# Gathering each run of 128 edges once in the three graph-attention passes of a GNN

## The reference, cut to what matters

```python
def _L1_gnn_ref(h, W, att, src, dst):
    z = jnp.einsum('nd,hdf->nhf', h, W)                 # 4 heads of 64
    es, ed = ...                                        # one score per node and head
    e = jax.nn.leaky_relu(es[src] + ed[dst], SLOPE)
    e = jnp.where(e == 0.0, NEG, e)
    m = jax.ops.segment_max(e, dst, num_segments=N)
    ex = jnp.exp(e - m[dst])
    denom = jax.ops.segment_sum(ex, dst, num_segments=N)
    alpha = ex / safe
    out = jax.ops.segment_sum(alpha[:, :, None] * z[src], dst, num_segments=N)

def _gat_layer(x, src, dst, W, a_src, a_dst, b, num_nodes):   # L2a: 4 heads, L2b: 1 head
    h = (x @ W).reshape(num_nodes, H, C)
    logits = jax.nn.leaky_relu(al_s[src] + al_d[dst], 0.2)
    alpha = _segment_softmax(logits, dst, num_nodes)
    out = jax.ops.segment_sum(h[src] * alpha[:, :, None], dst, num_segments=num_nodes)
```

## Time and profile before

| what | value |
|---|---|
| time, median of three runs | 3641.38 us (3639.26 to 3641.59) |
| the profiled execution: span of its instructions | 3626.7 us |
| time outside the span, by the difference | 14.7 us |
| instructions | 45,558 |
| VectorE (DVE), GpSimd (POOL) busy | 1987.0 us (55%), 2230.6 us (62%) |
| ScalarE (ACT) busy | 1393.1 us (38%) |
| gathers: L1, L2a, L2b together (L690 from t_z) | 1248, mean 984 ns |
| gathers of L3, of L0 | 416, 392 |
| moved by DMA | 389.14 MB, mean 107 GB/s |
| place loads (`dsthot`, four passes) | 416 of 128 KB |

### The profile page before, as it was taken

One profiled execution on the slowest core, in us unless ns is written; L12 is line 12 of the kernel. 1 busy time (PEld: TensorE's weight loads), 2 busy tenths in 40 slices (PEclk: granted clock), 3 DMA queues, 4 the chain that ended last, 5 costly groups with the idle time before them and its releaser, 6 DMA issues.

```text
span 3626.7 us, 45558 instructions
## 1 busy us (share of the span) xinstructions
PE 2379.2 (66%) x9551; PEld 1641.7 (45%) x9551; DVE 1987.0 (55%) x7379; ACT 1393.1 (38%) x3670; POOL 2230.6 (62%) x2460
## 2 busy tenths in 40 slices
PE   5655556838777774667777624554556588888888
PEld 2323334724444442344444424444454356555567
DVE  4554446536666673566666813333345366666677
ACT  2444544413333343333333513333343244444444
POOL 5666663566676657666766356666644366666636
PEclk7677677955666677666666755555555789999999
DMA  6656654234444423344444122222212255555411
GB/s 198 176 173 169 172 173 135 63 107 113 114 115 115 114 68 101 108 114 114 116 115 113 26 44 45 47 47 45 47 36 74 74 154 154 155 155 154 148 53 49
DMA packets 247934, 389.14 MB, mean 107 GB/s; under 512 B 58944, under 2 KB 161366, under 8 KB 247673
## 3 DMA queue, kind: packets, MB, share of 16 engines
q0 software_dynamic: 92032, 230.64, 24.6%
q1 hardware_dynamic: 155641, 155.59, 14.0%
HBM read 331.11 MB, written 54.91 MB: 106 GB/s over the span
## 4 chain that ended last, share of the span: by engine, by line
PE 39%; issue 21%; DVE 15%; another core or an unknown queue 14%; POOL 4%; ACT 3%; DVEq 2%; DMA 1%; SPq 0%; POOLq 0%; ACTq 0%
PE PS L1798 20%; PE PS L1719 6%; PE PS L1690 4%; DVE ACC L1323 3%; PE PS L1852 3%; POOL work L690 2%; DVE ACC L1090 1%; DVE work L1294 1%; PE PS L1776 1%; POOL rstd L579 1%; DVEq L376 1%; PE PS L1835 1%; PE PS L1748 1%; PE PS L1769 1%
## 5 line engine op out<-in xcount | busy, mean ns | idle before, releaser
L690 POOL DMA_INDIRECT work<-t_z,srcK x1248 | 1228.2, 984 | 610.8 <-issue 302.5
L1798 PE MATMUL PS<-work,M 128*128 128x260 f32 (+3 forms) x3328 | 1303.0, 512 | 447.6 <-issue 229.0
L1798 PEld LDWEIGHTS PS<-work,M 128*128 128x128 f32 x3328 | 757.4, 270 | 672.1 <-issue 480.2
L1323 DVE TENSOR_TENSOR ACC<-ACC,PS 128x260 f32 (+3 forms) x1614 | 588.7, 365 | 212.7 <-PE PS L1798 117.6
L2026 ACT ACTIVATE M<-iota,dloc 128x128 f32<-128x128 f32 x1248 | 396.9, 389 | 665.3 <-PE PS L1798 308.4
L690 POOL DMA_INDIRECT work<-t_x,srcK x416 | 394.0, 947 | 269.5 <-PE PS L1798 142.2
L690 POOL DMA_INDIRECT work<-in_x,srcTile x392 | 374.8, 956 | 212.2 <-issue 103.7
L1690 PE MATMUL PS<-work,M 128*128 x832 | 313.0, 519 | 240.8 <-issue 120.0
L1690 PEld LDWEIGHTS PS<-work,M 128*128 128x128 f32 x832 | 187.5, 250 | 361.5 <-issue 338.6
L1294 DVE TENSOR_TENSOR work<-work 128x256 f32<-128x256 f32 x800 | 329.1, 412 | 22.4 <-issue 14.2
L1719 PE MATMUL PS<-Y,w 128*128 x832 | 282.3, 425 | 72.2 <-issue 34.8
(11 more groups left out here) (266 smaller groups left out, 2928.9 us busy)
## 6 DMA issues: line engine op xcount, KB each, us to landing
work<-t_dhot SPq DMA_DIRECT2D x416, 128.0 KB
t_hot<-M SPq DMA_DIRECT2D x104, 256.0 KB
M<-t_hot SPq DMA_DIRECT2D x104, 256.0 KB
work<-t_z,srcK POOLq DMA_INDIRECT x1248
t_dhot<-work SPq DMA_DIRECT2D x104, 128.0 KB
work<-t_edge SPq DMA_DIRECT2D x104, 64.0 KB
work<-t_x,srcK POOLq DMA_INDIRECT x416
t_z<-Y SPq DMA_DIRECT2D x50, 130.0 KB, 2.0
```

Source lines behind the costliest of these rows:

```text
L690: pool.indirect_dma_start(out=slots[:, j, 0:width], out_offset=None, in_=table[:, :], in_offset=bass.IndirectOffsetOnAxis(ap=sources[:, k: ...
L1323: ins = vec.tensor_tensor(sums, sums, PS[k % SUMS[stage]][:, 0:cols], ALU.add)
L1798: mm(PS[k % n][:, 0:cols], M[:, k % (4 * G), :], slots_of[:, k % RING[stage], 0:cols], start=True, stop=True)\
```

## The change

- Each tile is gathered once in L1, L2a and L2b: 392 gathers a pass in place of 416, with the index table of tiles (`srcTile`) that L0 already uses. The ring of 48 slots now holds tiles.
- Rows stay raw in the ring. The tile's slot of a step is data, so VectorE, ScalarE and GpSimd load 16 slot numbers of a group into registers (`load_rows`, table `rowI`), read the row through them, and write the scaled row to a place of its own: one of three rows `sent` (where the weights w1 and w2 lay), or of 12 in the last 32 steps of L1 and L2a. Whoever writes such a row waits for the sum that read it (`wait_sent`). The weights of the softmax and the highest logits get tiles of their own (`alphas`, `tops`), and VectorE copies a step's highest logits into the sent row (`put_tops`), for which TensorE waits at each step of L2a and L2b.
- The source scores of a group are copied by ScalarE from the 16 rows into a tile (`take_sources`), after it has loaded the number of the last quad of tiles that the group needs; VectorE's second logit operation waits for that copy in place of the landing.
- SP passes on the landing of each four tiles (`relay_tiles`, tiles_ready) and, nine quads behind, that four slots are free (tiles_freed), once the steps in a table (`freeI`) are scaled. GpSimd waits for the latter once in four gathers.
- ScalarE issues the loads of `dsthot`, which SP did.
- A row is now 4 scores and four parts of 64 features and a one (264 wide), or 1 score and one part (66). The weighted ones give the denominators, so they need no fade of their own. The self-loop of L2a writes to `joined`.
- The setup makes the tables: four matmuls and one for `freeI`, and some seven small VectorE operations.

```diff
         slotI = Yf[0:1, late + PADDED + STEPS:late + PADDED + 2 * STEPS].bitcast(I32)
...
+        SENDS, SENDS_LATE = 3, 12
...
+        sent = w12[:, 0:SENDS * (SENT + HEADS)].rearrange("p (s c) -> p s c", s=SENDS)
...
-        WIDTH = {"L0": D, "L1": D, "L2a": D, "L2b": HID, "L3": D}
-        EXTRAS = {"L1": HEADS, "L2a": 2 * HEADS, "L2b": 2, "L3": 1}
+        WIDTH = {"L0": D, "L1": SENT, "L2a": SENT, "L2b": PART, "L3": D}
+        EXTRAS = {"L1": 0, "L2a": HEADS, "L2b": 1, "L3": 1}
+        TOPPED = ("L2a", "L2b")
...
+        def load_rows(eng, g):
+            _, values = nc.values_load_multi_w_load_instructions(
+                rowI[0:1, GS * g:GS * (g + 1)], engines=(eng.engine,), min_val=0, max_val=RING["L1"] - 1,
+                skip_runtime_bounds_check_because="the table was made from the steps' numbers")
+            return values
...
+        def sent_row(stage, k):
+            late = k - (STEPS - HELPED)
+            if late < 0 or stage == "L2b":
+                return sent[:, k % SENDS, :]
+            j = late % SENDS_LATE
+            return ring[:, FREE_SLOT + j, :] if j < SENDS_LATE - SENDS else sent[:, j - (SENDS_LATE - SENDS), :]
...
+        def wait_sent(eng, stage, k):
+            late = k - (STEPS - HELPED)
+            if late < 0 or stage == "L2b":
+                if k >= SENDS:
+                    eng.wait_ge(step_summed.sem, step_summed.at(stage, k - SENDS + 1))
...
+                eng.wait_ge(row_scaled.sem, row_scaled.at(stage, STEPS - HELPED))
...
+        LOT = each_of(SUMMING, G)
+        GATHERS = {**each_of(SUMMING, PADDED), "L3": STEPS}
...
+                sources = srcK if stage == "L3" else srcTile
...
-                    elif k >= many:
+                    elif k >= many and stage == "L3":
                         pool.wait_ge(step_summed.sem, step_summed.at(stage, k - many + 1))
+                    elif k >= many and k % G == 0:
+                        pool.wait_ge(tiles_freed.sem, tiles_freed.at(stage, (k - many) // G + 1))
...
+            def relay_tiles(stage):
+                for q in range(QUADS):
+                    landed(sp, stage, G * q)
+                    sp.sem_inc(tiles_ready.sem, 1)
+                    m = q - BEHIND
+                    if 0 <= m < FREED:
+                        steps = sp.value_load(freeI[0:1, m:m + 1], min_val=1, max_val=STEPS)
+                        sp.wait_ge(row_scaled.sem, steps + row_scaled.at(stage, 0))
+                        sp.sem_inc(tiles_freed.sem, 1)
...
-                        if c >= 4 and stage == "L3":
+                        if c >= 4:
                             sp.wait_ge(dsthot_made.sem, dsthot_made.at("L3", c - 3))
-                        elif c >= 4:
-                            sp.wait_ge(picked.sem, picked.at(stage, G * (c - 3)))
                         sp.dma_start(dsthot[:, c % 4, :], t_dhot[:, c * ROW:(c + 1) * ROW])\
                             .then_inc(dsthot_moved[c % 4].sem, 16)
...
+            sp.wait_ge(slots_made.sem, 3)
+            relay_tiles("L1")
+            store("L1", [(t_z2, lambda b, v: at_block(Y, b)[:, HEADS:BODY + SENT])], 1)
...
-                        landed(dve, stage, GS * g)
+                        dve.wait_ge(sources_taken.sem, sources_taken.at(stage, g + 1))
                         previous(1)
-                        ins = vec.tensor_tensor(by_step(L), by_step(A), ring[:, slot:slot + GS, width:width + heads], ALU.add)
...
+                def put_tops(k):
+                    g, i = divmod(k, GS)
+                    if i == 0:
+                        dve.wait_ge(tops_put.sem, tops_put.at(stage, g + 1))
+                    wait_sent(dve, stage, k)
+                    vec.tensor_copy(sent_row(stage, k)[:, width:width + heads], tops[:, g % 2, i * heads:(i + 1) * heads])\
+                        .then_inc(tops_sent.sem, 1)
                 def scale(k):
-                    j = k % RING[stage]
-                    if k % GS == 0:
-                        dve.wait_ge(alphas_put.sem, alphas_put.at(stage, k // GS + 1))
+                    g, i = divmod(k, GS)
+                    if i == 0:
+                        placed[0] = load_rows(dve, g)
+                        dve.wait_ge(alphas_put.sem, alphas_put.at(stage, g + 1))
+                    if helper(stage, k) != "vector":
+                        return
+                    wait_sent(dve, stage, k)
+                    row, o = ring_row(placed[0][i])[:, heads:heads + width], sent_row(stage, k)[:, 0:width]
                     if heads > 1:
-                        z = ring[:, j, 0:width].rearrange("p (h f) -> p h f", h=heads)
-                        ins = vec.tensor_tensor(z, z, ring[:, j, width:width + heads].unsqueeze(2)
-                                                .to_broadcast([P, heads, width // heads]), ALU.mult)
+                        ins = vec.tensor_tensor(o.rearrange("p (h f) -> p h f", h=heads), row.rearrange("p (h f) -> p h f", h=heads),
+                                                alphas[:, g % 2, i * heads:(i + 1) * heads].unsqueeze(2)
+                                                .to_broadcast([P, heads, PART]), ALU.mult)
                     else:
-                        ins = vec.tensor_scalar(ring[:, j, 0:width], ring[:, j, 0:width], ring[:, j, width:width + 1],
-                                                None, ALU.mult)
+                        ins = vec.tensor_scalar(o, row, alphas[:, g % 2, i:i + 1], None, ALU.mult)
                     ins.then_inc(row_scaled.sem, 1)
...
-                            d = sums[:, width:width + heads]
-                            vec.tensor_tensor(d, d, fade[:, 0:heads], ALU.mult).then_inc(sums_faded.sem, 1)
-                            dve.wait_ge(sums_faded.sem, sums_faded.at(stage, 2 * g))
+                            dve.wait_ge(sums_faded.sem, sums_faded.at(stage, g))
...
+                        elif early and 0 <= t - SOFAR < STEPS:
+                            if topped:
+                                put_tops(t - SOFAR)
                             scale(t - SOFAR)
...
+                    if topped:
+                        pe.wait_ge(tops_sent.sem, tops_sent.at(stage, k + 1))
...
+                    row = xring[:, k % RING[stage], 0:cols] if stage == "L3" else sent_row(stage, k)[:, 0:cols]
+                    mm(PS[k % n][:, 0:cols], M[:, k % (4 * G), :], row, start=True, stop=True)\
...
-                slots_of = xring if stage == "L3" else ring
...
-                sc.activation(slots_of[:, slot:slot + GS, width:width + heads],
-                              PS[6][:, 0:R].rearrange("p (h i) -> p i h", h=heads), ACT.Copy)\
+                place = xring[:, slot:slot + GS, width:width + 1] if stage == "L3" else\
+                    alphas[:, g % 2, 0:R].rearrange("p (i h) -> p i h", h=heads)
...
+                def load_places(c):
+                    if c >= CHUNKS:
+                        return
+                    if c >= 4:
+                        act.wait_ge(picked.sem, picked.at(stage, G * (c - 3)))
+                    sc.dma_start(dsthot[:, c % 4, :], t_dhot[:, c * ROW:(c + 1) * ROW]).then_inc(dsthot_moved[c % 4].sem, 16)
+                def take_sources(g):
+                    quad = act.value_load(quadI[0:1, g:g + 1], min_val=0, max_val=QUADS - 1)
+                    placed = load_rows(act, g)
+                    if g > 1:
+                        act.wait_ge(logit_ops.sem, logit_ops.at(stage, LOGIT_OPS[stage] * (g - 1)))
+                    act.wait_ge(tiles_ready.sem, quad + tiles_ready.at(stage, 1))
+                    for i in range(GS):
+                        last = sc.activation(taken(g, heads)[:, i, :], ring_row(placed[i])[:, 0:heads], ACT.Copy)
+                    last.then_inc(sources_taken.sem, 1)
...
+                for c in range(8):
+                    load_places(c)
+                    if c == 3:
+                        take_sources(0)
                 for g in range(NG):
+                    load_places(4 * g + 8)
                     spread_hots(stage, 4 * g)
                     spread_hots(stage, 4 * g + 1)
...
                     spread_hots(stage, 4 * g + 2)
                     spread_hots(stage, 4 * g + 3)
+                    load_places(4 * g + 11)
+                    if g + 1 < NG:
+                        take_sources(g + 1)
...
-                        j = k % RING[stage]
+                        if k % GS < 4:
+                            placed = load_rows(act, g)
+                        i = k % GS
                         act.wait_ge(alphas_put.sem, alphas_put.at(stage, g + 1))
+                        wait_sent(act, stage, k)
                         for h in range(heads):
-                            z = ring[:, j, h * HID:(h + 1) * HID]
-                            last = sc.activation(z, z, ACT.Copy, scale=ring[:, j, width + h:width + h + 1])
+                            last = sc.activation(sent_row(stage, k)[:, h * PART:(h + 1) * PART],
```

(2 more changed lines are left out.)

190 lines of the change are left out of this document (124 added, 66 removed).

## The result

The changed kernel takes 3950.4 us (median of four runs, 3933.0 to 3963.3) against 3640.3 us, a ratio of 1.086 with a 95% interval of 1.084 to 1.088: 310 us slower, where 85 us were forecast. The profiled execution has a span of 3954.2 us. The chips differ too (the kernel before takes 3635 to 3668 us on them), so every run is told as its ratio to the kernel before on the same chip; 0.1% is 3.6 us.

What follows compares the result with a forecast made beforehand. The prediction took exchanges between engines, with late steps and TensorE reports, to bound the kernel more than one engine's work. Its terms, -25 + 40 + 9 + 20 + 30 + 20 - 8 = +86 on 3641, gave 3725 us, range 3590 to 3870.

Steps and rivals of the forecast that it cites:

- Gathers, -25: GpSimd's 72 fewer gathers in the three passes: taken as 25 us saved, between 0 and 106.
- a rival with -106: Gathers set the pace of the three attention passes: 106 us saved, 3589 with additions; chance 0.28.
- Copies, +49: VectorE's second logit operation waits for ScalarE's source-score copies: raw 360 + 9 us, mostly hidden, taken as 40 and 9.
- Row numbers, +20: VectorE's register loads before each group's first scaling: 86 us raw, 20 taken, since TensorE is ahead.
- Highest logits, +30: VectorE's 832 copies into sent rows in L2a and L2b: 125 us raw, 30 taken.
- Three sent rows, +20: Scaling waits for the sum three steps back, where only the add did: 0 to 123 us, 20 taken.
- Place loads, 0: SP's 312 place loads move to ScalarE, which has room: 100 us of its time, nothing added to the sum.
- Slots freed by fours and at scaling: Ring slots come free by fours and at scaling instead of the sum: said to offset one another, nothing added.
- Setup, 0 to 3: A few small operations added in the setup: 0 to 3 us, taken as 0.
- the first rival: Gathers set the pace; about 5 more tail steps in each pass, +16 us; 3589 in all; chance 0.28.
- exposed in full: VectorE's wait for ScalarE's copies shows entirely, +360 + 9 us, 3977 in all; chance 0.10.
- All four marks named for a right forecast: ScalarE waits in some 75 groups, steps beside gathers at 1.5 us or more, longer GpSimd pauses, L2a slower than L1.

Runs made afterwards that it cites:

- e1: The kernel before without the gathers that fetch a tile a second time, 75 in the three passes: 0.974, 96 us less.
- e3: Like c3, but GpSimd waits for the sum of a tile's last step instead of its scaling: 0.983.
- e2: Like c3, but each row is scaled where it lies and its slot freed by its last sum: 0.983.
- c3: Like c2, but slots freed tile by tile at the scaling, without SP: 1.003 of the kernel before.
- c2: Changed kernel without source-score and highest-logit copies, VectorE's row numbers fixed, five or twelve sent rows, setup gathers held; slots still freed by fours through SP: 1.018.
- b1: Changed kernel with ScalarE's copies early and GpSimd's 15th gather of L0 held until TensorE reports its setup table products: 1.040.
- c1: Like b1, but GpSimd waits for the scaling of each tile's last step itself, tile by tile, without SP: 1.015.
- a3: Changed kernel with ScalarE's source-score copies moved ahead of the third and fourth one-hot chunk and place load: 1.040, 168 us less.
- b4: The kernel before with 23 gathers left out of each of three passes, the last of each group: 0.975, 93 us less for 69 gathers.
- c4: The kernel before with GpSimd holding back the ninth gather of L3 until the 25 query blocks are done: 0.997.
- a4: Changed kernel with VectorE taking its 16 row numbers of each group from the program instead of loading them: 1.079, 26 us less.
- b3: Changed kernel with copies early, without the 832 copies of the highest logits and TensorE's wait for them: 1.039.

## Why the prediction was wrong, point by point

Two steps of the sum failed towards too little. The wait for the copies was taken as covered but for 49 of 369 us, and cost 168 to 196. The way in which slots come free was put at nothing without a bound ("these offset one another"), and cost 129. The gathers' term failed the other way, 25 us saved in place of 96. The steps from the best case to the changed kernel, each from runs told above (0.1% is 3.6 us):

| step | ratio | us |
|---|---|---|
| fewer gathers alone (e1, three fewer than the change has) | 1.000 to 0.974 | -96 |
| tables, tiles in place of steps, the tail (e3, e2) | to 0.983 | +33 |
| slots freed by scaling, singly (c3) | to 1.003 | +73 |
| by fours, through SP (c2) | to 1.018 | +56 |
| early copies, highest logits, row numbers, three rows (b1) | to 1.040 | +79 |
| copies late, and setup not held (changed kernel) | to 1.086 | +168 |

Each row holds for this order alone: the fours and SP cost 56 us with the other additions off, and 90 with them on (b1 to c1). The last two rows can't be parted to the microsecond: a3, without the hold, also gave 1.040, on another chip, while the hold moved L1's start by 22 us.

- *Gathers, -25.* This term was mis-sized by a factor of four, and its reason was the wrong one. That VectorE does not wait for a landing was read as "the gathers are early". But leaving gathers out of the kernel before shortens it by their full pace (b4, e1). TensorE's reports come in GpSimd's pauses: of the 54 waits of over 3 us for TensorE, or for what the trace calls remote, in L1's long stretch of the kernel before, on VectorE and ScalarE, 33 end in the pauses, which are 13% of the time. That count alone does not say which holds up which, because GpSimd waits for TensorE there too and 30 of the 33 end within 0.5 us of its next gather; the held gathers of b1 and c4 do. A group then lasts 16 gathers and a pause, and the one pace of three passes, put down to a rival with -106, was the row to go by.
- *Copies, +49.* Raw wait 4.8 us a group, measured 5.2: right, though in other parts (16 copies 1.96 us, not 3.0). The discount failed. Of 369 us 49 were kept, and taking the wait away gave 168 to 196. The cover that was named, TensorE's rows in hand and waits for reports that run out together with this one, is there by half (403 us of standing, 196 us of time) and not by seven eighths. That the reports wait for a pause and not for time would explain it; no run shows that.
- *Row numbers, +20:* 26 measured. *Highest logits, +30:* 0 to 15. *Three sent rows, +20:* none. Its sign came true all the same: the adds' idle time went from 212.7 us (L1323) to 26.7 (L1434), and the scaling (L1407) has 120.7, so the wait changed its place and not its size. *Place loads, 0:* none.
- *Slots freed by fours and at scaling, "offset one another":* the step that failed worst, since no bound was set on it. They do not offset one another, they add up: 129 us, 73 for the scaling and 56 for the fours through SP, most of it in GpSimd's pauses.
- *Setup, 0 to 3:* L1 starts 26 us later. TensorE's last table product ends 6 us later than in the kernel before (35.1 us against 29.1), and its report comes only behind the last of 44 gathers. With the gathers held L1 starts early again, though no gain in the time was measured (b1). In the setup of the kernel before the same wait is 13 us, 7 of them behind the products' end.
- *Tail:* 54 sums behind L1's last gather in place of 48, as the first rival had it.

The rival "exposed in full" gave 3977, near the 3950 measured, but by 360 for the copies and nothing for the slots; its number was right by chance. All four marks named for a right forecast are there (waits for ScalarE of some us a group, 1.67 us a step beside gathers in L1, longer pauses, L2a slower than L1), and they do not tell the sizes apart. One mark against the copies' term is there too: the 16 copies take much under 3 us.

The 33 us between e1 and e2, which ran on the same chip, lie mostly in the tails: by the two traces 21 us there (55, 56 and 52 sums against 49, 50 and 45), 5 in the fills, 4 in the long stretches and some 5 before L1's first gather. Left open is how the parts of the 79 us in b1 share, beyond a4 and b3. Why gathers that follow one another hold up TensorE's reports was not found. The bytes do not look like the cause, since L2b moves a quarter as many at the same pace.

## What to carry to other kernels

- Where one engine streams work and others exchange steps, look at *when* waits end and not only at who is named: if they end in the streaming engine's pauses, that engine may set the pace, however early its results lie ready. Leaving out a part of the stream in the old kernel tells its worth in one run, ahead of any rebuilding.
- A new wait is not covered by an engine's other waits only because these are as long: here half of it was. Ask for the earliest place in the issuing engine's order: here moving 16 copies behind another operation gave back 168 us.
- Freeing a buffer earlier or in larger lots is a change of the stream's rhythm, and wants a bound of its own; here freeing at the scaling made the kernel slower, and so did the fours and the detour through SP together.

## What the runs showed of the hardware

- While GpSimd issues indirect gathers one behind another, TensorE's completions reach the other engines late by its recorded ends (which are modelled, so that a late matmul and a late report can't be told apart). In L3 it is by more the longer the row of gathers is: 0.55 us some 7 us into it, 2.4 at 15, 4.5 at 26, 5.1 at 37 us (c4), up to 15.7 us an exchange of two engines in L3's fill and 38 us in the setup of the changed kernel. Some 4 to 12 us behind the last gather they are prompt again, at 0.4 to 0.7 us. The Trainium skill (Perfetto Trace Analysis, DMA Instruction — SWDGE (GPSIMD)) says that the end of such an instruction in a trace is that of writing its descriptors, not of the data's landing; a lag behind the last gather's record is then no surprise, its growth before it is.
- The length of the row is not all. In the fill of L1 of the kernel before, some 23 us behind the first gather, VectorE gets on 0.04 us behind the ends of L1757 and L1764, TensorE having stood for 16 us; a few matmuls later it gets on 12.6 us behind that of L1769. And late in a row an exchange with six matmuls comes every 16.1 us (L1852 and L1835, L3's fill) and one with two every 4.9 us (L1721, c4), some 2.5 us a matmul both times. So the lateness goes with the matmuls too.
- A gather of 128 rows left out of the kernel before was worth 1.28 (e1) and 1.34 us (b4) of its time, beside a pace of 1.25 us in a row of gathers (0.95 and 0.30). The record of one is 1.00 us with rows of 1040 bytes (L1) and 0.94 with 260 (L2b).
- Sixteen ScalarE copies of 128x4 take 1.96 us, and sixteen scaling operations of 128x64 in the earlier trace rows 3.91 us.
